# A four-layer graph network on one Trainium2 core: each edge tile gathered once in the two plain passes, wait counts taken from tables, and no bounds checks on loaded offsets

## The reference

```python
x = layernorm(x + L0(x, src, dst, ...))   # sum of x[src]*norm over dst, then a small MLP with gelu
x = layernorm(x + L1(x, src, dst, ...))   # relu scores by edge type, softmax over dst, weighted sum
x = layernorm(x + L2(x, src, dst, ...))   # sum of x[src] over dst, then a small MLP with relu
x = layernorm(x + L3(x, edge_attr, src, dst, ...))   # 4-head attention with an edge term
# the sums over edges, in all four:
agg = segment_sum(feature[src], dst, num_segments=N)
# with softmax (L1, L3):
m = segment_max(e, dst); ex = exp(e - m[dst]); out = segment_sum(ex/denom[dst] * z[src], dst)
```

## Time and profile before

| what | value |
|---|---|
| median of 3 runs | 12,608.17 us (12,603.52 to 12,621.22) |
| the profiled execution's own time | 12,556.69 us |
| its span, on which all times of rows count | 12,555.0 us |
| busy POOL / PE / ACT / DVE | 6,450.9 / 4,294.8 / 3,446.0 / 1,628.9 us |
| setup | 0 to 271 us |
| plain pass 1, node stage | 271 to 2,727, to 2,862 us |
| attention pass 1 | 2,862 to 6,142 us |
| plain pass 2, node stage | 6,142 to 8,942, to 9,067 us |
| attention pass 2 | 9,067 to 12,555 us |

### The profile page before, as it was taken

The page is one execution under the profiler, slowest core; times in us unless marked ns, Lnnn a source line. Parts: engine busy times, 40 slices in busy tenths (PEclk is TensorE's granted clock), DMA queues, the critical chain, the costliest instruction groups (busy, mean ns, idle before and its releaser), DMA issues. The chain is left out here.

```text
span 12555.0 us, 93986 instructions
## 1 busy us (share of the span) xinstructions
PE 4294.8 (34%) x19065; PEld 3850.4 (31%) x19066; DVE 1628.9 (13%) x3883; ACT 3446.0 (27%) x9383; POOL 6450.9 (51%) x6784
## 2 busy tenths in 40 slices
PE   6233333352222232232244444444512222222222
PEld 5233332341222222222244444444412222222222
DVE  6000000013010110110100000000221111121113
ACT  1333333342222222222223223233312222222222
POOL 1666666656445445445355555555454444444442
PEclk6555555555555555555555555555555555555555
DMA  3111111112000000000111111111210111000110
GB/s 90 23 22 22 22 23 22 22 40 63 18 17 19 17 17 19 17 17 19 27 38 41 41 40 38 41 42 41 53 38 20 20 21 20 20 20 19 21 20 18
DMA packets 333875, 360.12 MB, mean 29 GB/s; under 512 B 172933, under 2 KB 205783, under 8 KB 330425
## 3 DMA queue, kind: packets, MB, share of 16 engines
q0 software_dynamic: 217552, 231.94, 9.4%
q1 hardware_dynamic: 116254, 127.34, 3.2%
HBM read 314.78 MB, written 46.51 MB: 29 GB/s over the span
## 5 line engine op out<-in xcount | busy, mean ns | idle before, releaser
L1037 POOL DMA_INDIRECT rows_a<-table,idx_c_a x3320 | 3166.1, 954 | 3380.4 <-ACT neg_c_a L999 2388.2
L839 POOL DMA_INDIRECT rows_l<-table,idx_c_l x3320 | 3140.1, 946 | 2349.8 <-ACT neg_c_l L793 1264.0
L587 PE MATMUL acc_l<-rows_l,hot_l 128*128 128x65 f32 x6640 | 1638.4, 419 | 2075.8 <-ACT hot_l L743 1226.6
L587 PEld LDWEIGHTS acc_l<-rows_l,hot_l 128*128 128x128 f32 x6640 | 1510.0, 328 | 2215.4 <-issue 2182.3
L587 PE MATMUL acc_a<-msg_a,hot_a 128*128 128x66 f32 (+1 forms) x6640 | 1612.1, 426 | 699.9 <-issue 520.7
L741 ACT ACTIVATE dist_a<-iota,neg_c_a 128x128 bf16<-128x128 f32 x3320 | 1050.9, 387 | 2664.3 <-remote 2286.5
L587 PEld LDWEIGHTS acc_a<-msg_a,hot_a 128*128 128x128 f32 x6640 | 1476.6, 328 | 833.0 <-issue 829.5
L1221 PE MATMUL work_a<-ident,tail_a 48*1 48x48 f32 (+3 forms) x140 | 32.7, 234 | 3410.9 <-DVE tail_a L1099 2844.2
L1221 PEld LDWEIGHTS work_a<-ident,tail_a 48*1 48x1 f32 (+3 forms) x140 | 10.8, 77 | 3439.6 <-issue 3439.6
L741 ACT ACTIVATE dist_l<-iota,neg_c_l 128x128 bf16<-128x128 f32 x3320 | 1049.9, 386 | 13.9 <-PE acc_l L587 8.5
L792 ACT COPY idx_c_l<-src_tl 128x16 int32 (+1 forms) x208 | 42.3, 204 | 3429.0 <-PE acc_l L587 1756.6
(11 more groups left out here) (258 smaller groups left out, 2499.2 us busy)
## 6 DMA issues: line engine op xcount, KB each, us to landing
rows_l<-table,idx_c_l POOLq DMA_INDIRECT x3320
rows_a<-table,idx_c_a POOLq DMA_INDIRECT x3320
feat<-edge_attr SPq DMA_DIRECT2D x25, 1125.0 KB
feat<-edge_attr SPq DMA_DIRECT2D x25, 937.5 KB
table<-stage SPq DMA_DIRECT2D x49, 260.0 KB
spread<-zero SPq DMA_DIRECT2D x12, 832.0 KB
starts_l<-spread SPq DMA_DIRECT2D x2, 3328.0 KB
we_v<-edge_s_l SPq DMA_DIRECT2D x1, 3328.0 KB
```

The lines of the kernel that those rows point to most:

```text
L587: return nc.tensor.matmul(acc[:, bass.ds(at, row.shape[-1])], hot, row, start=False, stop=True, skip_group_check=True)
L839: pool.indirect_dma_start(rows[:, s, k, 0:D], None, table, bass.IndirectOffsetOnAxis(idx_c[:, s, k:k + 1], 0))\
L1037: pool.indirect_dma_start(rows[:, u, k, 0:row], None, table, bass.IndirectOffsetOnAxis(idx_c[:, u, k:k + 1], 0)).then_inc(gathered[u], 16)
```

## The change

It has five parts.

1. **Plain passes gather tiles, not visits.** `idx_c` comes from a new table over tiles, `src_tt`, so POOL issues 1,612 gathers in a pass and no longer 1,660. `rows` is a ring of BODY = 64 tiles. The matmul takes its rows at a place in the ring that is loaded into a register, as the offset in `acc` is.
2. **Waits from tables.** PE loads, for each chunk of visits, how far the two semaphores `gathered[0]` and `gathered[1]` must have come (`lands`, two values). ACT loads, for each chunk of tiles, how far `summed` must have come for the places to be free (`frees`, one value).
3. **The order on ACT.** It is the tile numbers of chunk c (`tiles`, with a wait for `freed` and for the gathers of the chunk two back), the marks of chunk c+1, and the one-hots of chunk c. The distance of three chunks is gone.
4. **No bounds checks** on the values that PE and ACT load, those of the attention passes (L1206) too. The load of DVE (L1143) keeps its own.
5. **Setup.** Three more loads of `src`, one cast, 13 transposes and one copy on ACT for `src_tt`; 17 more small operations on DVE for `off_i[:, 1]`, `land_i` and `free_i`; four more DMAs for the tables. POOL waits for `tiles_cast` before the edges are gathered.

```diff
-                rows = tsb(f"rows_{tag}", [P, SLOTS, CH, D + 1])
+                rows = tsb(f"rows_{tag}", [P, BODY, D + 1])
-                gathered = [sem(f"gathered_{tag}_{s}") for s in range(SLOTS)]
+                gathered = [sem(f"gathered_{tag}_{s}") for s in range(2)]
...
                     def _(act):
-                        def columns(i, s, first):
-                            c = i * SLOTS + s
+                        def tiles(i, s, first, n):
                             if not first:
-                                act.wait_ge(summed, 1 + i * (BODY // QUAD) + (s + 1 - SLOTS) * CH // QUAD)
-                            nc.scalar.copy(idx_c[:, s], src_tl[:, bass.ds(c * CH, CH)]).then_inc(chunk_ready, 1)
-                            nc.scalar.copy(neg_c[:, s], neg_tl[:, bass.ds(c * CH, CH)]).then_inc(chunk_ready, 1)
+                                freed = nc.values_load(frees[0:1, bass.ds((i - 1) * SLOTS + s + 1, 1)], engines=ACT_ONLY, min_val=2, max_val=1 + VU // QUAD,
+                                                       skip_runtime_bounds_check_because=BOUNDED)
+                                act.wait_ge(summed, freed)
+                            if not (first and s < 2):
+                                act.wait_ge(gathered[s % 2], 16 * CH * (i * (SLOTS // 2) + s // 2))
+                            nc.scalar.copy(idx_c[:, s, 0:n], src_tt[:, bass.ds(i * BODY + s * CH, n)]).then_inc(chunk_ready, 1)
+                        def marks(i, s):
+                            nc.scalar.copy(neg_c[:, s % SLOTS], neg_tl[:, bass.ds(i * BODY + s * CH, CH)]).then_inc(neg_ready, 1)
...
-                        AHEAD = SLOTS - 1
-                        def body(i, first, second):
+                        def body(i, first, last):
                             for s in range(SLOTS):
-                                columns(i, s, first)
-                                if s >= AHEAD:
-                                    hots(i, s - AHEAD, first)
-                                elif not first:
-                                    hots(i - 1, s - AHEAD + SLOTS, second)
+                                if not last or s == 0:
+                                    tiles(i, s, first, REST_T if last else CH)
+                                if not last or s < SLOTS - 1:
+                                    marks(i, s + 1)
+                                hots(i, s, first, REST_V if last and s == SLOTS - 1 else CH)
...
                     def _(pool):
-                                for k in range(end if last else CH):
-                                    pool.indirect_dma_start(rows[:, s, k, 0:D], None, table, bass.IndirectOffsetOnAxis(idx_c[:, s, k:k + 1], 0))\
-                                        .then_inc(gathered_last[k // QUAD * QUAD] if last else gathered[s], 16)
+                                for k in range(REST_T if last else CH):
+                                    pool.indirect_dma_start(rows[:, s * CH + k, 0:D], None, table, bass.IndirectOffsetOnAxis(idx_c[:, s, k:k + 1], 0))\
+                                        .then_inc(gathered[s % 2], 16)
...
                         def body(i, first, end):          # on PE
                             for s in range(SLOTS):
                                 _, at = nc.values_load_multi_w_load_instructions(
-                                    offs[0:1, bass.ds((i * SLOTS + s) * CH, CH)], engines=PE_ONLY, min_val=0, max_val=TOP)
-                                if not last:
-                                    pe.wait_ge(gathered[s], 16 * CH * (i + 1))
+                                    offs[0:1, bass.ds(c * CH, CH)], engines=PE_ONLY, min_val=0, max_val=TOP, skip_runtime_bounds_check_because=BOUNDED)
+                                _, place = nc.values_load_multi_w_load_instructions(
+                                    offs[1:2, bass.ds(c * CH, CH)], engines=PE_ONLY, min_val=0, max_val=(BODY - 1) * (D + 1),
+                                    skip_runtime_bounds_check_because=BOUNDED)
+                                _, landed = nc.values_load_multi_w_load_instructions(
+                                    lands[0:1, bass.ds(c, 1)].rearrange("o c n -> o (c n)"), engines=PE_ONLY, min_val=16 * CH, max_val=16 * CH * CHUNKS,
+                                    skip_runtime_bounds_check_because=BOUNDED)
+                                for n in range(2):
+                                    pe.wait_ge(one, 1)
+                                    pe.wait_ge(gathered[n], landed[n])
...
-                                    ins = add_visit(acc, at[k], hot[:, n % DEPTH], rows[:, s, k, :])
+                                    ins = add_visit(acc, at[k], hot[:, n % DEPTH], places[:, bass.ds(place[k], D + 1)])
...
                         def offsets(g, lo, size):         # attention passes
                             return nc.values_load_multi_w_load_instructions(
-                                offs[0:1, bass.ds(g * S + lo, size)], engines=PE_ONLY, min_val=0, max_val=TOP)[1]
+                                offs[0:1, bass.ds(g * S + lo, size)], engines=PE_ONLY, min_val=0, max_val=TOP,
+                                    skip_runtime_bounds_check_because=BOUNDED)[1]
```

More of the change, by code:

```diff
@@ L32 @@
 PE_ONLY = (mybir.EngineType.PE,)
+ACT_ONLY = (mybir.EngineType.Activation,)
 P = 128
@@ L50 @@
 DEPTH = 32
+CHUNKS = -(-T // CH)
+REST_T = T - (CHUNKS - 1) * CH
+VCHUNKS = -(-VU // CH)
+REST_V = VU - (VCHUNKS - 1) * CH
 QUAD = 4
@@ L536, in _ @@
                         last.then_inc(begun_used, 1)
+                    pe.wait_ge(consts, 5)
+                    pe.wait_ge(tiles_cast, 1)
+                    for g in range(G):
+                        last = nc.tensor.transpose(turned[:, g * P:(g + 1) * P], src_f[:, g, :], ident[:])
+                    last.then_inc(tiles_turned, 1)
                     count(1)
-                    pe.wait_ge(consts, 5)
+                    pe.wait_ge(tiles_kept, 1)
                     pe.wait_ge(rows_ready, 1)
@@ L576, in build @@
         TOP = (NG - 1) * BANK + (BPB - 1) * AW
+        BOUNDED = "the table is worked out from a block number clamped to 0..NB - 1"
         def zero_sums(acc, summed):
@@ L795, in hots @@
-                        def hots(i, s, first, end=CH):
-                            act.wait_ge(chunk_ready, 2 * (i * SLOTS + s + 1))
-                            for k in range(0, end, QUAD):
-                                n = s * CH + k
-                                if not (first and n < DEPTH):
-                                    act.wait_ge(summed, 1 + i * (BODY // QUAD) + (n - DEPTH) // QUAD + 1)
-                                one_hots(act, neg_c[:, s, k:k + QUAD], dist, hot, n % DEPTH, dist_ready, i * (BODY // QUAD) + n // QUAD, hot_ready)
@@ new lines, in hots @@
+                        def hots(i, s, first, n):
+                            act.wait_ge(neg_ready, i * SLOTS + s + 1)
+                            for k in range(0, n, QUAD):
+                                at = s * CH + k
+                                if not (first and at < DEPTH):
+                                    act.wait_ge(summed, 1 + i * (BODY // QUAD) + (at - DEPTH) // QUAD + 1)
+                                one_hots(act, neg_c[:, s, k:k + QUAD], dist, hot, at % DEPTH, dist_ready, i * (BODY // QUAD) + at // QUAD, hot_ready)
@@ L816, in _ @@
-                        with act.Fori(2, ITERS) as i:
+                        with act.Fori(1, ITERS - 1) as i:
                             body(i, False, False)
-                        for s in range(1, SLOTS):
-                            hots(ITERS - 1, s, False, CH if s < SLOTS - 1 else CH - (V - VU))
+                        body(ITERS - 1, False, True)
                         if degrees:
@@ L832, in body @@
                         def body(i, first, end):
-                            for s in range(SLOTS):
-                                want = held(pool, 2 * (i * SLOTS + s + 1))
+                            last = end < CH
+                            for s in range(1 if last else SLOTS):
+                                want = held(pool, i * SLOTS + s + 1)
                                 pool.wait_ge(one, 1)
                                 pool.wait_ge(chunk_ready, want)
-                                last = s == SLOTS - 1 and end < CH
-                                for k in range(end if last else CH):
-                                    pool.indirect_dma_start(rows[:, s, k, 0:D], None, table, bass.IndirectOffsetOnAxis(idx_c[:, s, k:k + 1], 0))\
-                                        .then_inc(gathered_last[k // QUAD * QUAD] if last else gathered[s], 16)
+                                for k in range(REST_T if last else CH):
+                                    pool.indirect_dma_start(rows[:, s * CH + k, 0:D], None, table, bass.IndirectOffsetOnAxis(idx_c[:, s, k:k + 1], 0))\
+                                        .then_inc(gathered[s % 2], 16)
```

(2 more changed lines are left out.)

80 lines of the change are left out of this document (62 added, 18 removed).

## The result

The changed kernel took 12,146.7 us (median of 4 runs, 12,131.5 to 12,158.9), the kernel before 12,609.7 (4 runs beside them, 12,603.5 to 12,621.2). The ratio is 0.9631, with an interval of 0.9615 to 0.9648: 463 us faster, where the sum of the forecast had 1,307. The gain is a third of the forecast one.

What follows compares the result with a forecast made beforehand. It took the time to lie in waits, PE's sequencer being slow under gather bursts and its counts late. 12,557 + 2 (setup) - 150 - 200 (plain passes) - 960 (attention) = 11,249 us; own range 10,700 to 11,900, 8-in-10 range 10,600 to 12,300.

Steps and rivals of the forecast that it cites:

- the attention part: Attention passes: removing checks from offset loads shortens 64 periods by 15 us each, -960 us.
- 22 us in place of 44: Attention groups: without checks PE's counts come after half the time, so DVE starts at 10,760 and not 10,782.
- The first rival: Counts come with the burst's end whatever PE issues; attention gives 130 to 250 us, total 12,190 to 12,310; chance 0.15.
- the slowness: PE's sequencer is slow under a gather burst, 0.70 us an instruction against 0.146, so its counts reach others late.
- 15 us a period: Attention passes: first message 13.5 us earlier plus 1.9 us from the tails, taken as 15 over 64 periods.
- the second transpose of the tails: Attention passes: the second load of offsets held this transpose; without checks it gives 1.9 us more a period.
- five hand-overs: Attention passes: PE-to-DVE hand-overs inside the slow stretch cost 1.6 us more each, about 8.5 us off the gain.
- 48 x 1.25 = 60 us: Plain passes: 48 fewer gathers at 1.25 us give 60 us less POOL in each pass.
- a quarter and a fifth less: Plain passes: PE issues fewer instructions, so waits shrink by 90 us in the first pass, 140 in the second.
- Setup: Ahead of the first plain pass: added tables and operations cost +2 us, bounds 0 and +10.
- The granted clock: All four passes: no step moves it from 0.50, the lower of two levels (1.2 GHz).
- The rival of lost overlap: Plain passes: one-hots, loads and POOL's restart follow each burst, chunk period 35.5 us, total 13,810; chance 0.05.

Runs made afterwards that it cites:

- v5: Changed kernel, first plain-pass chunk waiting for its own gathers alone, attention bursts held until the previous group's scores are out; 11,074.7 against 12,569.5 us, ratio 0.8810.
- r: The changed kernel measured once more beside the kernel before; 8,951.7 against 9,009.1 us, ratio 0.9938.
- v6: Kernel before with no bounds checks on PE's loads and attention bursts held until the previous group's scores are out; 11,257.6 against 12,556.0 us, ratio 0.8966.
- e10: Changed kernel with checks back in plain pass 1, bursts held in attention pass 1, clearing behind each gather in attention pass 2; 11,478.4 beside 12,581.6 us.
- e12: Kernel before, checks included, with only attention bursts held until the previous group's scores are out; 11,670.9 us (one run).
- e4: Changed kernel with attention bursts held until the previous group's scores are out; 9,154.2 beside 9,004.4 us for the kernel before (one run).
- e1: Kernel before with only the attention passes' offset loads (L1206) unchecked; 8,991.4 against 9,004.4 us, ratio 0.9984.
- e8: Second run of the kernel of e5; 9,128.4 us beside 9,009.0 for the kernel before.
- e3: Changed kernel with four no-operation instructions on POOL behind each gather of the attention passes; 8,946.2 us.
- e5: Changed kernel with checks back in plain pass 1, bursts held in attention pass 1, clearing behind each gather in attention pass 2; 9,128.9 beside 9,025.5 us.
- e6: Kernel before with plain-pass gathers counted on two semaphores and ACT waiting for gathers two chunks back; 9,085.0 beside 9,009.0 us.
- e9: Kernel before, its four semaphores kept, with ACT waiting for gathers two chunks back before copying numbers; 12,615.2 beside 12,621.4 us.
- v4: Changed kernel with four gather semaphores, no ACT wait for gathers, first chunks waiting for what they use; 12,156.4 against 12,621.4 us, ratio 0.9631.

## Why the prediction was wrong

**The step that failed.** It is this sentence of the attention part: "Without them every turn goes to the counts, so these come after half the time, 22 us in place of 44". The checks didn't hold the counts. In the changed kernel PE had nothing to issue from 10,065 on, and the scores' count came at 10,121 all the same, 56 us later, where the forecast had it after 22. It follows the end of the burst, by 7.7 us before, 8.0 after, and 7.5 for another count in v5. I had read the agreement of two ends (the last slow instruction at 10,781.4, DVE at 10,782.2) as one holding the other; both followed a third thing, the burst. The first rival said so. The forecast also took the slowness for PE's own. It is not: in v5 DVE's register arithmetic takes 0.70 us, and ACT waits up to 4.5 us for a count that only ACT itself gives (the row is from after, 9000 to 12000; r has no such row):

```profile
ACT hot_a L801 <- remote: 156.9, 47, 4.5
```

**Its size.** The two passes gave 169 + 53 = 222 us, where the forecast had 960 and the first rival 130 to 250. Of the forecast's 15 us a period only the 1.9 for the second transpose of the tails was real: 2.01 to 0.42 is 1.6, and 1.6 is what 53 us over 33 periods are. In pass 1 a period gave more, 169 / 35 = 4.8, over the rival's 4. There the same wait fell from 4.9 to 0.42 us, 4.5 less, so that term is nearly all of it. Why it is longer there (one head, so a shorter softmax and less for the second load to lie beside) is argued from the order of the code. The forecast's sum has a small slip too: five hand-overs at 1.6 us are 8.0 us, not 8.5.

**The plain passes.** The gathers are 1,612 a pass, as the change says, and 48 x 1.25 = 60 us was the term for them; by 1.45 us a gather it would be 70. Pass 1 gave 65, but that it comes so near is luck, since it is a sum of three things. v6 shows the checks by themselves, 38 us a pass. That leaves 27 us in pass 1 for the 48 gathers and the new order together, so the new order takes back 33 to 43 of what the gathers give. I had given the waits a quarter and a fifth less (90 and 140 us), because PE issues fewer instructions. In pass 1 POOL's waits for ACT's copies didn't shrink at all: 329 us over 400 to 2600, where they were 312.

e10 shows the opposite side: with the checks the new order costs 105 us more than the old one with them (2,696 against 2,591), and without them 27 us less than the old one without them (2,526 against 2,553). So checks are worth 170 us in the new order and 38 in the old. That the new order, with its two more loads a chunk, has PE nearer to its limit would explain it; this is argued and not shown. Pass 2 gave 112 us: 38 for the checks and 74 for the rest, where the gathers alone are 60 to 70. The same code took 2,729 to 2,827 us there in other runs, so this size is uncertain by some 50 us.

**What was right.** Setup moved by 1 us (2 forecast). The granted clock stayed at its lower level, 0.50 to 0.51. The rival of lost overlap didn't come: the plain passes got shorter. The load of 16 values stayed at 1.10 us and the one of two values was 0.55, so the two loads that came are 1.65 us a chunk. The Trainium skill ("Runtime: NRT & Kernel Launch", section "Instruction fetch mechanics") would have 0.2 us a register, by which 18 are 3.6 us, an estimate from the page. That page's loads come from HBM, and `offs` lies in the on-chip memory SBUF, so weighing the row (0.07 us a value, 1.3 us for 18) over the page was right.

**Control instructions and queued matmuls.** The Trainium skill, "Advanced Engine Details and Errata", section "Sequencer Loop", has engine instructions read and queued while control instructions run. The trace after agrees with it: the load of the next offsets, which stands behind the transposes in the program, started at 10,061.3, and the transposes ran from 10,064.2. It should have had more weight than the coincidence of two ends.

**What stays open.** What fills up under closely issued gathers, if anything does, isn't known, nor whether their number under way or their rate brings it. Nor is it known why the same program meets the slowness in one measurement and not in another. Whether v5's hold is worth keeping depends on that. With the slowness the hold alone gained 7% (e12 against the kernel before), and v5 as a whole 12%. Without it the hold lost 2.3% (e4 against r).

## What to carry to other kernels

When two waits end together, look for a third event that both could follow (here the end of a burst) before pricing one as the cause of the other; a control is a stretch in which the supposed cause is short. A count that comes late costs what stands behind it, so move work ahead of the burst rather than making the late engine's work smaller: four lines that hold a burst until the scores are out gave 899 us on the kernel before, about twice what the change gave. And a POOL that gathers in bursts should be priced by burst and wait together (1.45 us a gather in plain pass 1), not by its issue alone (1.25). Before one slow engine is blamed, look whether the same kind of instruction is slow on the others.

## What the runs showed of the hardware

- One program had two levels: 9,004 to 9,026 us in the four measurements of e1 to e8 and r, and 12,556 to 12,621 in the five others (medians of the kernel before). On the second level register arithmetic under a burst of gathers takes 0.70 us on PE (0.146 elsewhere) and on DVE (0.040), and counts come late, those of ACT to itself by up to 4.5 us too. POOL waits 0.3 us between gathers on the first level and is busy for 51% of the span on the second.
- On the second level, bursts of 16, 32 and 48 gathers in plain pass 1 cost 1.44 to 1.48 us a gather with the wait behind them. With one gather at a time, 3.14 us apart, no register instruction of PE was slow.
- Four no-operation instructions behind a gather on POOL are hidden (e3, gathers 1.25 us apart as without them); a clearing of 128x64 is not (e5, 95 us more in a pass of 1,660 gathers).
- Counting gathers on two semaphores, with ACT waiting on them, made the gather after every 112 some 1.75 us late (e6 and the changed kernel, on both levels). With four semaphores, with that wait (e9) or without (v4), these gaps are gone.
